# Layer 3 of three images, in place of two, carries the sampling of the last image, each sampling unit in three parts at twelve places of three strips

## The reference, cut to what matters

```python
def _L2_conv_ref(x, ...):
    integ = jnp.cumsum(jnp.cumsum(x, axis=-1), axis=-2)
...
    area = area * scale
...
    A = _grid_sample_border_bilinear(integ, off_tl)
    Bt = _grid_sample_border_bilinear(integ, off_tr)
    Ct = _grid_sample_border_bilinear(integ, off_bl)
    D = _grid_sample_border_bilinear(integ, off_br)
    return (A + D - Bt - Ct) / area
...
def _edffn(x, w_in, w_dw, fft_w, w_out):
    h = jnp.einsum('bchw,oc->bohw', x, w_in)
    h = jax.lax.conv_general_dilated(h, w_dw, window_strides=(1, 1), padding='SAME', feature_group_count=2 * HID, ...)
    x1, x2 = jnp.split(h, 2, axis=1)
    h = jax.nn.gelu(x1, approximate=False) * x2
    y = jnp.einsum('bchw,oc->bohw', h, w_out)
...
    f = jnp.fft.rfft2(yp.astype(jnp.float32)) * fft_w
    yp = jnp.fft.irfft2(f, s=(P, P))
...
x = x + _L2_conv_ref(_gn(x), ...)
x = x + _L3_conv_ref(_gn(x), ...)
```

## Time and profile before

| | us |
|---|---|
| median of 3 runs | 29315.67 (29310.48 to 29318.21) |
| the profiled execution | 29288.99 |
| its span | 29286.8 |
| layer 3, image 0, with 64 units | 1662 |
| layer 3, image 1, with 64 units | 1662 |
| layer 3, image 2, no units | 1021 |
| layer 3, image 3, no units | 1021 |

### The profile page before, as it was taken

The page is one execution under the profiler, slowest core; times in us unless marked ns, Lnnn a source line. Parts: engine busy times, 40 slices in busy tenths (PEclk is TensorE's granted clock), DMA queues, the critical chain, the costliest instruction groups (busy, mean ns, idle before and its releaser), DMA issues. The chain is left out here.

```text
span 29286.8 us, 426241 instructions
## 1 busy us (share of the span) xinstructions
PE 25223.7 (86%) x148532; PEld 16664.0 (57%) x148532; DVE 15920.1 (54%) x23720; ACT 6983.5 (24%) x13095; POOL 9328.8 (32%) x8560
## 2 busy tenths in 40 slices
PE   1998888899988888999888889998888886667899
PEld 1775444657754446577544465775444645555677
DVE  5333444456656664566566645665666455555433
ACT  0332222113322221133222211332222111111222
POOL 0000000025544440255444402554444028788100
PEclk9999999799999997999999979999999798888999
DMA  3110000244422222444222224442222245555333
GB/s 93 39 39 22 16 16 15 78 112 100 101 68 60 61 62 75 113 99 101 72 61 61 62 79 112 99 99 71 62 61 62 76 115 125 117 121 126 79 73 74
DMA packets 834735, 2253.49 MB, mean 77 GB/s; under 512 B 255632, under 2 KB 507284, under 8 KB 709208
## 3 DMA queue, kind: packets, MB, share of 16 engines
q1 hardware_dynamic: 413856, 1309.70, 19.5%
q0 software_dynamic: 419840, 928.94, 12.5%
HBM read 1860.62 MB, written 385.13 MB: 77 GB/s over the span
## 5 line engine op out<-in xcount | busy, mean ns | idle before, releaser
L1628 POOL DMA_INDIRECT e_got<-table,e_idx x8192 | 9041.0, 1104 | 8074.6 <-DVE e_box L1668 5335.5
L1032 DVE TENSOR_TENSOR b_ym<-b_p_f,b_mask 128x304 f32<-128x304 f32 x2112 | 1001.0, 474 | 4200.9 <-PE b_p_f L864 4198.8
L975 ACT ACTIVATE b_ys<-b_p_in 128x304 f32<-128x304 f32 x2112 | 896.0, 424 | 8170.5 <-PE b_p_in L912 8170.4
L1046 DVE SCALAR_TENSOR_TENSOR b_acc<-b_z,b_dwc,b_acc 112x1024 f32<-112x1024 f32 x2112 | 2595.1, 1276 | 0.0
L283 PE MATMUL d_p<-d_xs,d_ws 125*96 125x512 f32 x9216 | 2484.7, 415 | 108.4 <-DVE d_xe L299 56.5
L871 PE MATMUL b_p_z<-const,b_ym 128*66 128x128 f32 (+2 forms) x12672 | 1866.8, 285 | 772.0 <-ACT b_z L963 772.0
L871 PEld LDWEIGHTS b_p_z<-const,b_ym 128*66 128x66 f32 (+2 forms) x12672 | 1671.8, 176 | 1364.0 <-ACT b_z L963 885.7
L495 PE MATMUL a_p_qk<-a_wst,a_stack 125*128 125x192 f32 x12288 | 2421.1, 333 | 26.1 <-issue 11.4
L1654 DVE TENSOR_TENSOR e_got<-e_got,e_wt 128x3072 f32<-128x3072 f32 x512 | 1712.8, 3345 | 1291.9 <-DMA e_got<-table,e_idx 654.0
L887 PE MATMUL b_p_conv<-b_z,b_diag_a 64*64 64x512 f32 x19008 | 2327.2, 611 | 96.1 <-DVE b_g_a L1061 96.1
L495 PEld LDWEIGHTS a_p_qk<-a_wst,a_stack 125*128 125x128 f32 x12288 | 2009.0, 190 | 123.8 <-ACT a_qh L603 80.3
(11 more groups left out here) (271 smaller groups left out, 40449.1 us busy)
## 6 DMA issues: line engine op xcount, KB each, us to landing
e_got<-table,e_idx POOLq DMA_INDIRECT x8192
a_stack<-in_xp SPq DMA_DIRECT2D x256, 387.0 KB
c_stack<-planes SPq DMA_DIRECT2D x256, 387.0 KB
d_stack<-planes SPq DMA_DIRECT2D x256, 387.0 KB
table<-i_acc SPq DMA_DIRECT2D x256, 384.0 KB, 2.3
b_x<-planes SPq DMA_DIRECT2D x132, 395.1 KB
b_xr<-planes SPq DMA_DIRECT2D x132, 395.1 KB
planes<-b_out SPq DMA_DIRECT2D x132, 395.1 KB
```

What stands on the lines that cost most here:

```text
L1032: dve.tensor_tensor(ym[k % 2][:], p_f[:, 0:NC], mask[:], ALU.mult).then_inc(masked, 1)
L1046: dve.scalar_tensor_tensor(out=a, in0=rows, scalar=dwc[0:M[D], D, k:k + 1], in1=a, op0=ALU.mult, op1=ALU.add).then_inc(chain, 1)
L1628: pool.indirect_dma_start(out=self.got[q][:, t, c * REC:(c + 1) * REC], out_offset=None, in_=self.flat, in_offset=bass.IndirectOffsetOnAxi ...
```

## The change

The 128 units are spread over 96 strips, those of images 0, 1 and 2 (`joint` is 3), and only image 3 runs without. A group of three strips holds one strip of boxes, four units. Every quarter of a strip (slots 1, 3, 5, 7) is a **place**, so a group has twelve, and each unit takes three: `weigh` at the first, `halve` at the second, `finish` at the third. PE turns a unit at the start of the strip behind the one in which it was finished: one, one and two units in the three strips. The loops take six strips a turn in place of four or eight.

POOL gathers unit by unit, each with its own wait for the addresses: 46 units in the block of image 0, 43 (46 to 88) in that of image 1, 39 in that of image 2 (`ahead`). At the end of images 0 and 1 it runs up to four units past those that DVE has taken. The buffers, the 16 DMAs of a unit and its DVE instructions are the same as before.

```diff
+    def gather_unit(self, pool, v, at):
+
+        slot, j = divmod(at, 2)
+        q = at % self.nb
+        pool.wait_ge(self.idx_loaded[slot], (self.listed[slot] + v + 1) * 16)
+        pool.sem_inc(self.turn_sem, 1)
+        pool.wait_ge(self.used, self.n0 + v * (2 * self.ni) + at - self.nb + 1)
+        pool.sem_inc(self.turn_sem, 1)
+        for t in range(4):
+            for c in range(4):
+                col = (j * 4 + t) * 4 + c
+                pool.indirect_dma_start(out=self.got[q][:, t, c * REC:(c + 1) * REC], out_offset=None, in_=self.flat,
+                                        in_offset=bass.IndirectOffsetOnAxis(ap=self.idx[slot][:, col:col + 1], axis=0)
+                                        ).then_inc(self.gathered[q][t // 2], 16)
+
+    def gather_units(self, pool, lo, hi):
+
+        per = 2 * self.ni
+        first, last = -(-lo // per), hi // per
+        for n in range(lo, min(hi, first * per)):
+            self.gather_unit(pool, n // per, n % per)
+        if last > first:
+            with pool.Fori(first, last) as v:
+                for at in range(per):
+                    self.gather_unit(pool, v, at)
+        for n in range(max(lo, first * per, last * per), hi):
+            self.gather_unit(pool, n // per, n % per)
...
+    def part(self, dve, e, i, j, k):
+        if k == 0:
+            self.weigh(dve, e, i, j)
+        if k == 1:
+            self.halve(dve, e, i, j)
+        if k == 2:
+            self.finish(dve, e, i, j)
...
+        PER = 6
+        LEAD, TURNS = 2, (S - 8) // PER
...
-            for r in range(4):
+            for r in range(LEAD):
                 step(0, r, first + r, True, r > 0, True)
-            if S > 8:
-                with eng.Fori(1, S // 4 - 1) as v:
-                    for r in range(4):
-                        step(v, r, first + v * 4 + r, True, True, True)
-            for r in range(4):
-                step(S // 4 - 1, r, first + S - 4 + r, True, True, r < 3)
-            step(S // 4, 0, first + S, False, True, False)
-
-        def unit(v, r, j):
-
-            return half * U + v * 2 + r // 2, r % 2, j
-
-        def turned(v, r, j):
-
-            return unit(v, r - 1, j) if r else unit(v - 1, 3, j)
+            if TURNS:
+                with eng.Fori(0, TURNS) as v:
+                    for r in range(LEAD, LEAD + PER):
+                        step(v, r, first + v * PER + r, True, True, True)
+            for r in range(LEAD + TURNS * PER, S):
+                step(0, r, first + r, True, True, r < S - 1)
+            step(0, S, first + S, False, True, False)
...
+        def group(v, r):
+
+            g, third = divmod(b * S + r, 3)
+            return v * 2 + g, third
+
+        def part(v, r, k):
+
+            e, third = group(v, r)
+            u, what = divmod(4 * third + k, 3)
+            return e, u // 2, u % 2, what
+
+        def turned(v, r):
+
+            e, third = group(v, r - 1)
+            return [(e, u // 2, u % 2) for u in ((0,), (1,), (2, 3))[third]]
...
-                    e = v * 4 + r // 2 + half * U
-                    if boxes and load:
-                        boxes.blended(sp, e, k)
-                        if more > 1:
-                            boxes.load_idx(sp, e + 2, k, r % 4)
-                        boxes.load_aux(sp, e + 1, k)
+                    if boxes:
+
+                        e, i = group(v, r)
+                        i -= 1
+                        left = S - (b * S + r) // 3 - 1 if b == joint - 1 and r >= LEAD + TURNS * PER else 2
+                    if boxes and i >= 0:
+                        boxes.blended(sp, e, i)
+                        if left >= 2:
+                            boxes.load_idx(sp, e + 2, i, (b * S + r) // 3 % 2 * 2 + i)
+                        if left >= 1:
+                            boxes.load_aux(sp, e + 1, i)
...
+                    if boxes and i >= 0:
+                        boxes.store(sp, e, i)
+                        if left >= 1:
+                            boxes.load_x(sp, e + 1, i)
...
-                    boxes.gather(pool, half * U, (half + 1) * U)
+
+                    ahead = [4 * S * i // 3 + boxes.nb if i else 0 for i in range(joint)] + [4 * S]
+                    boxes.gather_units(pool, ahead[b], ahead[b + 1])
...
-                        for j in range(2):
-                            boxes.turn(pe, *turned(v, r, j), p_c[j])
+                        for unit in turned(v, r):
+                            boxes.turn(pe, *unit, p_c[unit[2]])
...
-                            for j in range(2):
-                                boxes.residual(dve, *turned(v, r, j), p_c[j])
-                        if boxes and front and i in (1, 5):
-                            boxes.blend(dve, *unit(v, r, i // 4))
+                            for unit in turned(v, r):
+                                boxes.residual(dve, *unit, p_c[unit[2]])
+                        if boxes and front and i % 2:
+                            boxes.part(dve, *part(v, r, i // 2))
...
-        for b in range(2):
-            layer3(env, p1, out, args("d_"), b, boxes, b)
+        for b in range(B - 1):
+            layer3(env, p1, out, args("d_"), b, boxes, B - 1)
         phase.close()
         fold_prep(env, "d", env.stats, [B - 1], env.box_stats, 4 * env.S)
-        for b in range(2, B):
-            layer3(env, p1, out, args("d_"), b)
+        layer3(env, p1, out, args("d_"), B - 1, joint=B - 1)
```

More of the change, by code:

```diff
@@ L1701, in residual, with layer3 @@
         dve.bn_stats(self.env.stats[:, ds(n - self.n0 + self.env.box_stats, 1), :].rearrange("p e k -> p (e k)"), rows).then_inc(self.stats_done, 1)
[L1704 removed]
+def layer3(env, src, dst, p, b, boxes=None, joint=0):
     nc, S = env.nc, env.S
@@ L1784, in _ @@
                 load_image(sp, src, b, 0, out[0], x_loaded0)
-                if boxes:
-                    boxes.load_first(sp, half * U)
+                if boxes and b == 0:
+                    boxes.load_first(sp, 0)
                 def strip(v, r, load, more):
-                    s, k = v * 8 + r, r % 2
+                    s, k = v * PER + r, r % 2
                     if load:
@@ L1810, in strip @@
                     sp.dma_start(dst[b, :, ds(s * SROWS, SROWS), :], out[k][1:CP, :, 1:1 + W]).then_inc(stored[k], 16)
-                    if boxes:
-                        boxes.store(sp, e, k)
-                        if load:
-                            boxes.load_x(sp, e + 1, k)
-                if S > 8:
-                    with sp.Fori(0, S // 8 - 1) as v:
-                        for r in range(8):
-                            strip(v, r, True, 2)
-                for r in range(8):
-                    strip(S // 8 - 1, r, r < 6, 2 if r < 4 else r < 7)
+                    if boxes and i >= 0:
+                        boxes.store(sp, e, i)
+                        if left >= 1:
+                            boxes.load_x(sp, e + 1, i)
+                for r in range(LEAD):
+                    strip(0, r, True, True)
+                if TURNS:
+                    with sp.Fori(0, TURNS) as v:
+                        for r in range(LEAD, LEAD + PER):
+                            strip(v, r, True, True)
+                for r in range(LEAD + TURNS * PER, S):
+                    strip(0, r, r < S - 2, r < S - 1)
                 for k in range(2):
                     sp.wait_ge(stored[k], ((b + 1) * U + 1) * 16)
-                if boxes:
-                    boxes.stores_done(sp, (half + 1) * U)
+                if boxes and b == joint - 1:
+                    boxes.stores_done(sp, S)
             if boxes:
@@ L1834, in _ @@
                     start(pe, sem, k)
-                if boxes and half == 0:
+                if boxes and b == 0:
                     boxes.first_credit(pe)
@@ L1867, in inverse @@
                         if boxes and h == 0:
-                            boxes.bank_free(pe, *turned(v, r, j))
+                            for unit in turned(v, r):
+                                if unit[2] == j:
+                                    boxes.bank_free(pe, *unit)
                         for t in range(4):
```

8 lines of the change are left out of this document (4 added, 4 removed).

## The result

The changed kernel takes 28547.98 us (median of 4 runs, 28512.5 to 28560.42) against 29313.53 us beside it (4 runs, 29310.48 to 29318.21): a ratio of 0.9737, 95% interval 0.972 to 0.9754. The forecast was 28435, its range 28260 to 28650. The time lies in the range, 113 us above the forecast, and 23 us above the band of 28345 to 28525 that the forecast's own case was given. The profiled execution took 28551.12 us, with a span of 28549.6.

A forecast was written before the change was run, and what follows sets the result against it. POOL's gathers were taken to bound images 0 and 1; at 26.35 us a unit, images of 1222, 1141, 1102 and 1020.4 us ended the span at 28406, so 28435 us was forecast, factor 0.970, 80% range 28260 to 28650.

The forecast's parts named there:

- the forecast's own case: Images 0 to 2: POOL's gathers remain the bound, at 25.6 to 27.1 us a unit; 28345 to 28525 us, chance 0.61.

The follow-up runs named there:

- e3: Changed kernel with the split undone: the whole blend of a unit stands at the first of its three places; 28445.85 us, ratio 0.9718.
- e4: Changed kernel with each of the three pieces behind the quarter's product instead of right behind the `lower` terms; 28424.13 us, ratio 0.9707.
- e9: Changed kernel with POOL gathering three units ahead across an image's end, not four, second time, on another chip; 33486.55 us, ratio 0.9877.
- e1: Changed kernel with image 3's weighing working on one of its 64 blocks, every gather and wait kept; 28197.5 us.

## What to carry to other kernels

Here a GpSimd gather that starts beside a row of VectorE instructions with both inputs in SBUF is held until the row's next pause, even one of 0.035 us. So count what runs without a pause, not instructions: cutting a long step into pieces gains only if the pieces do not lean on other steps of the same kind, and a step behind a long one costs little where a pause lies between them (0.54 us for the halving in e3). Where the engine that was never last becomes the last one, its distance to a barrier has to be asked for anew. And an order that is tuned to one engine's bound, here e3 and e4, can lose where the other engines are held up: compare such fine orders on more than one chip.

## What the runs showed of the hardware that I had not expected

- Two chips ran every one of these kernels, the one of before too, some 15% longer (33795 and 33947 us against 29287), with the same pace in stretches without POOL's gathers (e9: 872 us of PE work in 1000 against 871) and less work in those with them (760 against 991). The cause was not found.
- A held gather ends 0.81 to 0.84 us behind the end of a VectorE instruction with two SBUF inputs (470 of 495 in the changed kernel), and a pause of 0.035 us between two such instructions lets it through.
- 16 gathers take 26.8 us at 162 GB/s and 26.7 at 139: this much more traffic does not touch their pace.
- From POOL's last gather to the next block's first instruction pass 8.7 us at the end of image 0 and 10.0 at the end of image 1, in the changed kernel and in e1 to e4. What it consists of was not measured.
